# A decoder layer on one core: deferred projection rows, score-time query transposes, iterated roots, 16-bit attention weights

## The reference

```python
x = x + attention(layernorm(x))           # 16 heads of 64, four batches of 256 tokens, width 128
x = x + cross_attention(layernorm(x), ctx)  # 16 heads of 8, ctx has 1601 rows per batch, mask is 0 here
x = x + mixture(layernorm(x))             # 8 experts, two per token, gated products
# attention: q, k, v, scores, weights and outputs are truncated to multiples of 1/4096 (make_fxp)
attn = make_fxp(softmax(make_fxp(q @ k.T * scale)))
out = make_fxp(make_fxp(attn @ v) @ w_proj.T + b_proj)
# cross attention
weights = softmax(qh @ kh.T + mask); ctx_out = weights @ vh; relu(ctx_out @ wo_w.T + wo_b)
```

## Time and profile before

| what | value |
|---|---|
| median of 3 runs | 681.28 us (679.99 to 685.09) |
| the profiled execution | 678.65 us |
| its span, first to last instruction | 676.9 us |
| mean granted TensorE clock | 0.933 of full |
| busy in the span | PE 565.7, DVE 497.0, ACT 473.9, POOL 141.0 us |
| stage 1 / 2 / 3 / 4, roughly | 0 to 206 / 206 to 258 / 258 to 562 / 577 to 677 us |

### The profile page before, as it was taken

The page is one execution under the profiler, slowest core; times in us unless marked ns, Lnnn a source line. Parts: engine busy times, 40 slices in busy tenths (PEclk is TensorE's granted clock), DMA queues, the critical chain, the costliest instruction groups (busy, mean ns, idle before and its releaser), DMA issues.

```text
span 676.9 us, 13952 instructions
## 1 busy us (share of the span) xinstructions
PE 565.7 (84%) x5108; PEld 315.7 (47%) x5115; DVE 497.0 (73%) x896; ACT 473.9 (70%) x850; POOL 141.0 (21%) x215
## 2 busy tenths in 40 slices
PE   5799888988869468999889988999896894799992
PEld 3465555555548233333333333333331242799992
DVE  2578889888986977888878888888884433667662
ACT  3879999998983027778678875878674773577760
POOL 5001001000003433230125011500012106232332
PEclk9999999999999759999999999999996877699995
DMA  9822845723768427010641037000005001111103
GB/s 232 246 103 74 167 166 129 197 83 117 205 174 205 76 98 249 2 51 1 144 126 50 2 67 204 2 1 3 1 1 190 2 1 50 40 41 44 42 28 101
DMA packets 31669, 62.89 MB, mean 93 GB/s; under 512 B 4526, under 2 KB 21338, under 8 KB 31156
## 3 DMA queue, kind: packets, MB, share of 16 engines
q0 software_dynamic: 8000, 40.91, 22.9%
q1 hardware_dynamic: 22020, 20.31, 10.2%
q10 hardware_dynamic: 1584, 0.79, 0.4%
HBM read 42.29 MB, written 19.30 MB: 91 GB/s over the span
## 4 chain that ended last, share of the span: by engine, by line
PE 46%; DVE 20%; ACT 16%; DMA 8%; issue 7%; SPq 1%; POOL 0%; POOLq 0%; ACTq 0%; DVEq 0%
DVE smax L1684 13%; PE pair L1099 11%; PE pair L1074 6%; PE pair L1260 6%; ACT region_p L1340 5%; PE pair L1029 5%; PE pair L1248 3%; ACT region_p L1348 3%; ACT region_p L1438 2%; PE pair L929 2%; DMA region_b<-in_mask_Bx1xSxS_ff 2%; PE pair L916 2%; PE pair L900 2%; PE pair L1270 1%; ACT region_p L1326 1%
## 5 line engine op out<-in xcount | busy, mean ns | idle before, releaser
L1684 DVE TENSOR_REDUCE smax<-pair 128x2 f32<-128x1024 f32 x192 | 225.5, 1219 | 53.5 <-PE pair L1029 52.8
L1438 ACT ACTIVATE region_p<-pair 128x1024 f32<-128x1024 f32 (+3 forms) x277 | 217.7, 812 | 66.8 <-PE pair L1074 61.5
L1557 DVE SCALAR_TENSOR_TENSOR region_p<-region_p 128x1024 int16<-128x1024 int16 (+1 forms) x56 | 67.1, 1220 | 10.3 <-ACT region_p L1326 8.2
L1099 PE MATMUL pair<-region_p 128*32 128x256 f32 (+1 forms) x832 | 69.9, 410 | 0.5 <-ACT region_p L1445 0.4
L1099 PE MATMUL pair<-region_p,region_b 128*32 128x256 f32 (+1 forms) x832 | 66.5, 391 | 0.4 <-ACT region_p L1445 0.4
L1074 PE MATMUL pair<-region_b,region_k 59*128 59x256 bf16 (+1 forms) x416 | 54.7, 273 | 8.7 <-ACT region_p L1438 4.3
L1029 PE MATMUL pair<-region_k,region_b 56*128 56x512 bf16 (+1 forms) x256 | 44.3, 364 | 18.7 <-DVE smax L1684 17.5
L1340 ACT ACTIVATE region_p<-region_p 128x256 f32<-128x256 int16 x128 | 51.4, 413 | 0.0
L916 PE MATMUL pair<-ident,region_p 128*128 128x128 f32 x256 | 36.3, 287 | 11.8 <-DVE region_p L1590 11.8
L1260 PE MATMUL pair<-region_p 128*128 128x128 f32 x368 | 45.5, 277 | 0.0
L929 PE MATMUL pair<-region_p 128*64 128x256 f32 x256 | 34.7, 392 | 12.4 <-ACT region_p L1348 11.5
(11 more groups left out here) (244 smaller groups left out, 970.2 us busy)
## 6 DMA issues: line engine op xcount, KB each, us to landing
kimg<-region_k SPq DMA_DIRECT2D x56, 200.1 KB
region_k<-kimg POOLq DMA_DIRECT2D x8, 1400.9 KB, 18.1
region_b<-in_mask_Bx1xSxS_ff POOLq DMA_DIRECT2D x12, 800.5 KB, 7.6
region_p<-in_mask_Bx1xSxS_ff POOLq DMA_DIRECT2D x4, 800.5 KB, 12.9
region_k<-in_L_ffn_W POOLq DMA_DIRECT2D x3, 1024.0 KB, 9.5
xdisp<-region_x POOLq DMA_DIRECT2D x1, 2322.0 KB, 19.0
region_b<-in_ctx SPq DMA_DIRECT2D x3, 768.0 KB
xdisp<-region_x POOLq DMA_DIRECT2D x1, 2257.5 KB, 18.5
```

What stands on the lines that cost most here:

```text
L1099: last = pe.matmul(pair[3][32 * h:32 * h + 32, 512 + s % 2 * S:512 + (s % 2 + 1) * S], v_heads[b % 2][0:rows, t, c:c + 32], pT[0:rows, n / ...
L1438: act.activation(pT[0:rows, first // 3 % 2, k:k + size], home[0:rows, 0:size], ACT.Exp).then_inc(expt_made, 1)
L1557: return dve.scalar_tensor_tensor(out_, floor16, 0.0, floor16, ALU.is_lt, ALU.add)
L1684: last = dve.tensor_reduce(units[:, :, c // 3, c % 3], both, AX.X, ALU.max)
```

## The change

It has these parts.

1. **16-bit weights.** `make_attn` writes the rounded-down weight as a 16-bit integer (`attn16`) and no longer runs the extra pass over 1024 columns (L1590). PE transposes the integers as bf16 bit patterns with `identb`, and ACT's move reads them as integers. In the last head pair PE's transposes and DVE's weights come ahead of the mask flag's work.
2. **Later batches' output put off.** DVE does `attention_out` for batch 0 only. For batches 1 to 3 it just copies the projection out of PSUM (`out_move`), and starts on the maxima. The rest (truncate, residual, statistics, root, apply) runs in six pieces after pairs 19, 21, 23, 25, 27 and 29. PE projects the second part in two halves, one before and one behind the first transposes of queries, and the third between pairs 1 and 3.
3. **Fewer pairs ahead.** 18 pairs stand before event 0; two pairs per event follow until the old count is reached at event 2.
4. **Queries of batches 1 to 3 among scores.** PE's 16 transposes for each stand at events 30, 50 and 70, ACT's moves one event later, and the pair that takes the bank next waits for the move.
5. **Root by iteration.** The roots of the later batches and at `X2_AT` are made by DVE (a bit trick with `ROOT_MAGIC` and three rounds, 14 small chained operations), not by ACT.
6. **POOL's list.** The clamps of mask 0 go from DVE to POOL, the splits of groups 0 and 1 ahead of the split of the later queries, `Wg` and `Wl` behind the split of group 7, and `experts_load` waits until group 14's small transfer has landed.
7. **The last finish** is written into both arms of the `If`.

```diff
-LEAD = 22
+LEAD, FIRST = 22, 18
+def pairs_by(e):
+
+    return min(FIRST + 2 * (e + 1), LEAD + 3 * (e + 1) // 4)
+QUERIES_AT = (30, 50, 70)
+LATER_AT = (19, 21, 23, 25, 27, 29)
...
-                            last = pe.transpose(pair[1][:, c:c + 128], attn[:, b % 2, a:a + 128], ident[:, :])
+                            last = pe.transpose(pair[1][:, :].bitcast(BF16)[:, c:c + 128], attn16.bitcast(BF16)[:, b % 2, a:a + 128],
+                                            identb[:, :])
...
-                    last = dve.tensor_scalar(attn_h[:, b % 2, k * 256:(k + 1) * 256], expd[:, b % 2, k * 256:(k + 1) * 256],
+                    last = dve.tensor_scalar(attn16[:, b % 2, k * 256:(k + 1) * 256], expd[:, b % 2, k * 256:(k + 1) * 256],
                                              rnorm[:, k:k + 1], -0.5, ALU.mult, ALU.add)
-                chain.step(last)
-                dve.tensor_scalar(attn[:, b % 2, :], attn_h[:, b % 2, :], MAGIC, MAGIC, ALU.add,
-                                  ALU.subtract).then_inc(attn_made, 1)
+                last.then_inc(attn_made, 1)
...
+            def norm_root(tiles):
+
+                cut_ = slice(*tiles)
+                root, half, square = rstd[:, cut_], std[:, cut_], meanvar[:, cut_, 1]
+                chain.step(dve.tensor_scalar(half, var_eps[:, cut_], -0.5, None, ALU.mult))
+                chain.step(dve.tensor_scalar(root.bitcast(I32), var_eps[:, cut_].bitcast(I32), 1, None, ALU.logical_shift_right))
+                chain.step(dve.tensor_copy(square, root.bitcast(I32)))
+                chain.step(dve.tensor_scalar(square, square, -1.0, ROOT_MAGIC, ALU.mult, ALU.add))
+                chain.step(dve.tensor_copy(root.bitcast(I32), square))
+                for _ in range(3):
+                    chain.step(dve.tensor_tensor(square, root, root, ALU.mult))
+                    chain.step(dve.tensor_tensor(square, square, half, ALU.mult))
+                    chain.step(dve.scalar_tensor_tensor(root, square, 1.5, root, ALU.add, ALU.mult))
...
+            for t in range(2):
+                mask_clamp(0, t)
+            split_maxima(0)
+            split_maxima(1)
             pool.wait_ge(proj_mm, len(OUT_TILES))
...
+            def gates_load():
+
+                pool.wait_ge(qstack_made, B)
+                for n, w in enumerate((Wg, Wl)):
...
             def experts_load():
 
+                pool.wait_ge(shift_loaded, 32 * (GROUPS - 1))
...
             for s in range(1, GROUPS):
-                split_maxima(s)
+                if s > 1:
+                    split_maxima(s)
+                if s == 7:
+                    gates_load()
...
+                for later in range(1, B):
+                    if n == SLOT["queries", later]:
+                        pe.wait_ge(qstack_made, later + 1)
...
+                        if e in QUERIES_AT:
+                            b = QUERIES_AT.index(e) + 1
+                            pe.wait_ge(slot_done, SLOT["queries", b] - 1)
+                            queries_T(b, pair[SLOT["queries", b] % 2])
...
+            def last_finish():
+
+                finish_tiles(B - 1, 0, pair[2])
+                finish_tiles(B - 1, 1, pair[3][:, 0:256])
+                biases_T()
+                finish_tiles(B - 1, 2, pair[3][:, 256:512])
...
-                if e == X2_AT:
-                    std_of(5, FFN_TILES[0])
...
+                elif piece == 4:
+                    norm_root(LATER)
+                else:
+                    norm_apply(3, x1, LATER)
...
             attention_out(0)
-            attention_out(1)
-            attention_out(2)
+            out_move(1)
```

165 lines of the change are left out of this document (94 added, 71 removed).

## The result

| | changed kernel | kernel before |
|---|---|---|
| runs beside the first measurement | 701.19 us median of 4 (689.97 to 712.37) | 680.95 (679.99 to 685.09) |
| runs beside the experiments | 691.79 us median of 6 (679.41 to 696.99) | 679.51 median of 11 (676.02 to 685.63) |
| profiled execution, span | 699.31 us, 697.3 us | 678.65 us, 676.9 us |
| granted TensorE clock | 0.912 | 0.933 |

The ratio of the first measurement is 1.0209, 95% interval [1.0148, 1.0271]; of the second 1.0017 [0.9941, 1.0093]; both ratios leave out the changed kernel's slower runs, two of its four and four of its six. The forecast was 677.0 and at most 685. Two things have to be explained: a loss of 2% in the first measurement, where a small gain was forecast, and runs that lie 33 us apart where before's lie within 10.

The account below looks back on a forecast made before the run. No one engine bounds the run (PE 46% of the chain, DVE 20%, ACT 16%). Terms sum to 3.9 us gained, 678.65 to 674.7 profiled; with 2.6 for the runs' median 677.4, rounded to 677.0, range 662 to 685.

Parts of the forecast that it names:

- 16-bit weights, all of stage 1: Stage 1: faster transposes and no extra DVE pass gain 3.8 us in head pairs 0 to 6, 2.6 in the last.
- turn, pair 0: Turn to stage 3: without mask and batches 1 to 3, DVE starts pair 0 at 217.6, not 229.06.
- POOL's late split: Pair 43: POOL's longer list makes PE wait for group 2's split, costing 2.8 us, bounds 0 and 10.1.
- queries among scores: Events 30, 50, 70: each costs about 2.0 us, partly hidden under waits for small transfers; 4.7 us lost, bounds 2.5 to 8.7.
- Wg and Wl: Group 7: these loads delay its small transfer; PE stands 9.2 us, lower clock costs 3.9; 13.2 us lost, bounds 0 and 15.
- experts_load: Group 14: waiting for its small transfer returns 5.2 us of wait and 3.9 of lower clock; 9.1 us gained, bounds 6 and 11.
- root: At X2_AT: no ACT table loads and no lower clock behind them; 5.3 us gained, bounds 2 and 6.
- last finish: Behind the If: the finish runs ahead and the gap falls under DVE's normalization; 0.8 us gained, bounds 0.3 and 3.
- Batch 0's normalization, 2.6 us earlier than before, lets its queries through at 213.2: Turn to stage 3: earlier normalization releases batch 0's queries at 213.2, leading to pair 0 at 217.6.
- C: Rival: 16-bit weights and stage 3's start give about 2 us, not 3.8 + 5.6; total 684.8; chance 0.15.
- the four marks: Turn to stage 3: pair 0, first nmT, pair 18, end of pair 29; 213.8, 235.0, 239.5, 261.7, less 3.8 for stage 1.
- Rival A: Group 7's small transfer is served between the large ones, so the 13.2 us do not fall due; total 664.2; chance 0.22.

Follow-up runs that it names:

- b1: The kernel before with the 16-bit weights alone (mask flag's work behind the last weights); 677.62 us, 0.9913.
- f1: Changed kernel, three repairs: POOL's loads wait for ones (pads cleared first), mask 0 clamps behind group 0's split, Wg/Wl behind group 7's small transfer; 669.2 us, 0.9807.
- f2: f1 with group 2's split on POOL ahead of the clamp of mask 1; 665.0 us, 0.976.
- e4: Changed kernel with the loads of Wg and Wl waiting until group 7's small transfer has landed; 685.76 us.
- b4: b2 with experts_load behind group 14's small transfer and the last finish in both arms of the If; 663.62 us, 0.9753.
- b2: b1 with POOL waiting for the ones transfers and clearing the queries' pads ahead of its mask and key loads; 674.85 us, 0.9927.
- b3: b4 with the root at the last events by iteration on DVE, nothing deferred; 664.5 us, 0.9739.
- b5: b4 with DVE's two clamps of mask 0 behind the normalization of batches 1 to 3, as its last work ahead of pair 0; 662.2 us, 0.9751.
- after: The changed kernel's profiled execution, unrepaired; 699.31 us.
- e2: Changed kernel with POOL waiting for the ones transfers ahead of its mask and key loads; 686.0 us, 1.0082.
- b6: b5 with the root by iteration and PE's transposes, gates and ranks of the last events two events later; 661.9 us, 0.9719.
- f5: f2 with the clamps of mask 0 on DVE behind its split of batch 0, as in the kernel before; 668.12 us, 0.9794.

## Why the prediction was wrong

The profiled execution was forecast at 674.7 and took 699.3 us. By its own steps (plus is time gained):

| step | forecast | measured |
|---|---|---|
| 16-bit weights, all of stage 1 | +6.4 | +5.0 (b1), by ACT's last probe 3.6 to 8.6 earlier, mostly 7; the 16-bit writes kept the old speed (1.14 us for four) |
| turn, pair 0 | 213.8 | 231.64; 212.10 in f1 |
| POOL's late split | -2.8 | -2.7 (f1 against f2) |
| queries among scores | -4.7 | -6.3 (1.6, 2.6 and 2.1, f2 against before) |
| Wg and Wl | -13.2 | -11.5 (e4) |
| experts_load | +9.1 | +9.7 (b4 against b2) |
| root | +5.3 | none (b3 against b4); +2.7 by groups 14 and 15 of f2 (33.6) against b4 (36.3) |
| last finish | +0.8 | 0 to +1.7, by the stretch to the end |

**The step that failed** is "Batch 0's normalization, 2.6 us earlier than before, lets its queries through at 213.2", and with it "pair 0 starts at 217.6". Pair 0 came 17.8 us late, and the first exponential's scores with it. The sentence took the queries as following the normalization. They also need SP's ones, which I had not looked up because DVE never waited for them: in before they landed 0.4 us ahead of use. And stage 1, made shorter, moved the two issues together as well, since POOL's loads hang on ACT's last probe and SP's on the landing of the image stores: the lag shrank from 1.61 to 0.26 us, and the flight grew from 9.5 to 18.4. The work I moved to POOL came on top. The sum gives the clamps on POOL no price; beside them DVE's five operations took 9.0 us against 2.0, 7.0 more. And behind PE's stand of 17.73 us its projection took 5.77 us instead of 3.79, at the lower clock. Of the rivals none named either. C came nearest in that the turn's gain was gone, but for a reason that it didn't have.

**Up to pair 29 the deferral was modelled rightly**: with those two repaired, the four marks of f1 lie 1.7, 1.9, 1.8 and 2.6 us from the forecast ones. What I had not seen is that the end of pair 29 is not where the gain is to be read. It was 12.0 us earlier than before in f1, but group 1 ended 6.0 earlier, and after the queries of groups 2 and 4 only 1.2: b5, which puts nothing off, is 5.5 us ahead of f2 at the end of group 4. By the totals, 0.9751 [0.9704, 0.9799] against 0.976 [0.9713, 0.9807], the deferral is worth nothing that can be measured. The two differ in more than that (b5 has ACT's root, and its clamps are DVE's), but b3, which has the iterated root as well, is at 0.9739 [0.9682, 0.9795]; no run takes the deferral alone out of f2.

**Wg and Wl**: right in kind and near in size, with the split between wait and clock wrong (5.2 of wait, not 9.2). Rival A, that the small transfer is served between the large ones, was right on the order of service, and still wrong on the price: 11.5 us fell due. The Trainium skill, "DMA: Bandwidth & Descriptors", section on queues, rings and completion order, says that each DMA engine goes round its queues packet by packet. The landing at 406.2, three microseconds ahead of the weights' end, agrees with it, and so does the table of lags, which rises without a step; my reading of group 14 as "only when the large ones ended" does not. In these runs a small transfer was not blocked by the large ones, but stretched.

**The root** was mis-sized by the price of where it stands. The table loads did go. But DVE's 14 steps end 1.56 us after PE wants the rows, and behind such a wait the clock was at half for 20 us in b3 and for parts of 562 to 580 in after; in f2 it came back within 5 us. Group 15 took 25.8 us in b3, 22.5 in after, 18.4 in f2 and 17.4 in e2, so that this is a second thing that makes the time vary. I had taken the price of the lower clock off, and had not asked whether the new wait would call for it again. b6, without the wait, has the 5.2 us.

**The spread**: the interval of 662 to 685 was one for a kernel as steady as before. The changed kernel has two places that vary, the race for the ones (first exponential 257.23 and 253.10 in its two traces) and group 15 (22.5 and 18.4): 679.41 us is the changed kernel, too. In f2, where POOL waits and there is no race, the runs lie within 4.3 us, but in f1, where there is none either, within 11.2, so the race is not the whole of it.

## What to carry to other kernels

A wait of zero length is no slack: before making a stage shorter, list what each first instruction behind it waits for, when that landed or ended, and what that is issued behind; here the narrowest margin was 0.4 us, and the changed kernel waited 10.20 us in its place. When two engines issue transfers that compete, have the one with the large ones wait for the small one that somebody needs, and then look at which transfer has become the late one. Work moved from a busy engine to an idle one is free only if the two don't slow each other. When a run shows the number that a rival named, look also for the wait that the rival named: in f5 the number was there and the wait was not. And work put off is a loan from the engine that is full later.
